# Relation-typed messages in a graph kernel: one-hots as the standing operand, weighted rows split in two fp32r parts, sums turned before they are added

## The reference, cut to what matters

```python
def _L1_gnn_ref(h, weight, norm, src, dst, rel_type):
    transformed = jnp.einsum('ni,rio->rno', h, weight)   # 16 relations
    msg = transformed[rel_type, src] * norm              # one row of 256 per edge
    return jax.ops.segment_sum(msg, dst, num_segments=h.shape[0])
```

## Time and profile before

| | us |
|---|---|
| median of 3 timed runs | 4358.07 (4357.03 to 4358.71) |
| span of the profiled execution | 4602.8 |
| of it from 2428 to 3597, the stage that is changed | 1169 |

### The profile page before, as it was taken

The page is one execution under the profiler, slowest core; times in us unless marked ns, Lnnn a source line. Parts: engine busy times, 40 slices in busy tenths (PEclk is TensorE's granted clock), DMA queues, the critical chain, the costliest instruction groups (busy, mean ns, idle before and its releaser), DMA issues. The chain is left out here.

```text
span 4602.8 us, 88005 instructions
## 1 busy us (share of the span) xinstructions
PE 3885.9 (84%) x23733; PEld 3489.0 (76%) x23733; DVE 2976.4 (65%) x7006; ACT 2107.0 (46%) x4811; POOL 2125.1 (46%) x2102
## 2 busy tenths in 40 slices
PE   7899999999999988989995666667666699999993
PEld 6798898989889877987885655556556578888883
DVE  7698898989889876554332222222321488989888
ACT  3565565656556536763221000000000288989882
POOL 0455555555555501000006666666666167667671
PEclk9899999999999987999995555665655599999996
DMA  4466666656556610004443333333333123323225
GB/s 138 135 176 171 171 175 171 177 170 175 169 170 177 169 31 23 24 26 161 151 150 103 89 87 89 92 87 91 87 89 90 52 55 75 63 67 70 60 48 120
DMA packets 226998, 509.09 MB, mean 111 GB/s; under 512 B 51805, under 2 KB 94299, under 8 KB 220426
## 3 DMA queue, kind: packets, MB, share of 16 engines
q0 software_dynamic: 116736, 313.66, 24.7%
q1 hardware_dynamic: 106389, 187.30, 14.6%
q10 hardware_dynamic: 3679, 5.79, 0.4%
HBM read 434.08 MB, written 72.49 MB: 110 GB/s over the span
## 5 line engine op out<-in xcount | busy, mean ns | idle before, releaser
L685 POOL DMA_INDIRECT big<-table,e_idx x784 | 751.2, 958 | 1049.6 <-DVE e_idx L721 649.0
L356 POOL DMA_INDIRECT big<-table,e_idx x784 | 767.0, 978 | 856.9 <-issue 304.1
L703 PE MATMUL psum<-e_near_hot,big 128*128 128x64 f32 x3136 | 621.9, 371 | 377.6 <-issue 361.9
L703 PEld LDWEIGHTS psum<-e_near_hot,big 128*128 128x128 f32 x3136 | 616.7, 292 | 391.7 <-issue 386.7
L2191 POOL DMA_INDIRECT g_S<-gsrc,g_idx x512 | 588.8, 1150 | 274.8 <-issue 157.8
L748 DVE TENSOR_TENSOR big<-big,psum 128x128 f32 x196 | 56.6, 289 | 801.9 <-remote 489.6
L435 ACT ACTIVATE e_hT_hi<-psum 128x256 fp32r<-128x256 f32 x784 | 300.2, 383 | 593.9 <-PE psum L375 513.1
L468 DVE TENSOR_TENSOR big<-psum,big 128x512 f32<-128x512 f32 x784 | 539.4, 688 | 45.5 <-issue 22.8
L386 PE MATMUL psum<-e_w_hi,e_hT_hi 128*128 128x256 f32 x1568 | 509.8, 325 | 0.3 <-issue 0.3
L386 PE MATMUL psum<-e_w_hi,e_hT_lo 128*128 128x256 f32 x1568 | 443.7, 283 | 0.0
L386 PE MATMUL psum<-e_w_lo,e_hT_hi 128*128 128x256 f32 x1568 | 440.7, 281 | 0.0
(11 more groups left out here) (397 smaller groups left out, 9090.5 us busy)
## 6 DMA issues: line engine op xcount, KB each, us to landing
big<-in_attr_t SPq DMA_DIRECT2D x392, 128.0 KB
g_rest<-gpart SPq DMA_DIRECT2D x128, 256.0 KB
big<-table,e_idx POOLq DMA_INDIRECT x1568
table<-C SPq DMA_DIRECT2D x26, 896.0 KB
table<-n_rows SPq DMA_DIRECT2D x24, 896.0 KB
experts<-g_region SPq DMA_DIRECT2D x15, 560.0 KB
g_S<-gsrc,g_idx POOLq DMA_INDIRECT x512
table<-big SPq DMA_DIRECT2D x25, 224.0 KB
```

Source lines behind the costliest of these rows:

```text
L356: pool.indirect_dma_start(G[:, j % 2, q, :], None, table, bass.IndirectOffsetOnAxis(idx[:, j, q:q + 1], 0)).then_inc(s[f"G_in{j % 2}{q}"], 16)
L685: pool.indirect_dma_start(G[:, j % n, q, :], None, c.table1, bass.IndirectOffsetOnAxis(idx[:, j, q:q + 1], 0)).then_inc(s[f"G_in{j % n}"], 16)
L703: last = pe.matmul(acc[:, b, :], G[:, j % n, q, b * 128:(b + 1) * 128], onehot[:, q, :], start=q == 0 and (b == 0 or s is sems[1]), stop=q ...
```

## The change

It changes only the first pass of `stage_relations` (the attention class gives up its own buffers for two weight matrices and takes them in `big`).

- The roles in the matmul are exchanged. The one-hot stands (128 edges x 64 nodes) and the gathered rows move (256 columns). Both are in fp32r, and as one fp32r value does not hold a weighted row exactly enough, the row is split in two: `hi` and `lo`. There are 8 matmuls a sup again (4 tiles x 2 parts).
- ScalarE makes `hi` = row x norm rounded to fp32r, 4 activations of 128x256 a sup. VectorE makes `lo` = row x norm - `hi`, 4 `scalar_tensor_tensor` of 128x256. Both have two buffers.
- The one-hot is no longer multiplied with `norm`; VectorE makes it two sups ahead, in 4 buffers.
- The sum now comes as nodes x features (64x256). ScalarE copies it out of PSUM (`rows`), TensorE turns it with two transposes, and VectorE adds the turned sum to `agg`.
- A slot of `G` is free again when `lo` has been made, not when the sup has been multiplied.
- `norm` is copied to a small tile (`scale`) with the indices.

The core of the diff:

```diff
-    NEAR_SLOTS, FAR_SLOTS, ACCS = 7, 2, 4
-    LEAD = 4
+    SLOTS, HOTS, FAR_SLOTS, FAR_BANKS = 7, 4, 2, 4
+    LEAD = 2
...
+        hi, lo = (sb(n, [128, 2, SUP, D], F32R) for n in ("hi", "lo"))
+        near_hot = sb("near_hot", [128, HOTS, SUP, WIN], F32R)
+        rows = c.C[0:WIN, 0:2, :]
...
+        def near_pool(pool):
...
+                    pool.wait_ge(s["low"], sup + 1)
...
+        def near_scalar(act):
+            def high(a):
+                k, j, sup = a
+                act.wait_ge(G_in[j % SLOTS], (k * (SUPS // SLOTS) + j // SLOTS + 1) * 16 * SUP)
+                act.wait_ge(s["sup_done"], sup + HOTS - 1)
...
+                for q in range(SUP):
+                    last = act.activation(hi[:, j % 2, q, :], G[:, j % SLOTS, q, :], ACT.Identity, scale=scale[:, j, q:q + 1])
+                last.then_inc(s["high"], 1)
+
+            def evict(a):
+                k, j, sup = a
+                act.wait_ge(s["sup_done"], sup + HOTS + 1)
+                act.wait_ge(s["turned"], sup + 1)
+                act.activation(rows[:, j % 2, :], acc(j), ACT.Copy).then_inc(s["rows"], 1)
             def step(k, v, beside=None):
+                if at(k, v - 2):
+                    evict(at(k, v - 2))
+                if at(k, v):
+                    high(at(k, v))
...
+        def near_tensor(pe):
+            def products(a, beside):
+                k, j, sup = a
+                pe.wait_ge(s["hot_ready"], sup + 1)
+                pe.wait_ge(s["low"], sup + SLOTS + 1)
+                pe.wait_ge(s["rows"], sup + 1)
+                for q in range(SUP):
+                    for n, part in enumerate((hi, lo)):
+                        last = pe.matmul(acc(j), near_hot[:, j % HOTS, q, :], part[:, j % 2, q, :],
+                                         start=q == 0 and n == 0, stop=q == SUP - 1 and n == 1)
...
+            def turn(a):
+                k, j, sup = a
+                pe.wait_ge(s["rows"], sup + 3)
+                pe.wait_ge(s["added"], sup + 1)
...
+                for b in range(KB):
+                    last = pe.transpose(turned(j)[:, b, :], rows[:, j % 2, b * 128:(b + 1) * 128], c.ident[0:WIN, 0:WIN])
+                last.then_inc(s["turned"], 1)
+            def step(k, v, beside=None):
+                if at(k, v):
+                    products(at(k, v), beside)
+                if at(k, v - 1):
+                    turn(at(k, v - 1))
...
+        def near_vector(dve):
...
+            def low(a):
+                k, j, sup = a
+                dve.wait_ge(s["high"], sup + 1)
+                for q in range(SUP):
+                    last = dve.scalar_tensor_tensor(out=lo[:, j % 2, q, :], in0=G[:, j % SLOTS, q, :], scalar=scale[:, j, q:q + 1],
+                                                    in1=hi[:, j % 2, q, :].bitcast(F32), op0=ALU.mult, op1=ALU.subtract)
+                last.then_inc(s["low"], 1)
+            def add_window(a):
+                k, j, sup = a
+                dve.wait_ge(s["turned"], sup + 3)
+                dve.wait_ge(s["added"], sup + 2)
...
+                dve.tensor_tensor(cols, cols, turned(j), ALU.add).then_inc(s["added"], 1)
+            def step(k, v, beside=None):
+                if at(k, v - 2):
+                    add_window(at(k, v - 2))
+                if at(k, v + LEAD):
+                    hots(at(k, v + LEAD))
+                a = at(k, v)
+                if a:
+                    low(a)
```

More of the change, by code:

```diff
@@ L649, in at, with far_loop, near_loop, acc @@
             return k, v, k * SUPS + v
[L651 to L676, removed]
+        def far_loop(eng, step, first):
+            for v in range(first, SUPS):
+                step(0, v)
+            with eng.Fori(1, NB - 1) as k:
+                for v in range(SUPS):
+                    step(k, v)
+            for v in range(SUPS + 1):
+                step(NB - 1, v)
+        def near_loop(eng, step, first, after, aside):
+            for v in range(first, SUPS):
+                step(0, v)
+            with eng.Fori(0, NT // GROUP) as g:
+                for v in range(SUPS):
+                    step(g + 1, v, lambda: aside(v % TURN, g, v // TURN, (g + 1) * SUPS + v))
+            for v in range(SUPS + after):
+                step(NB - 1, v)
+        def acc(j):
+            return c.ps[4 + j % 2][0:WIN, 0:D]
+        def turned(j):
+            return c.ps[6 + j % 2][:, 0:KB * WIN].rearrange("p (b n) -> p b n", b=KB)
+        def near_pool(pool):
             with pool.Fori(0, NB) as k:
@@ new lines, in far_acc, with far_pool @@
+        def far_acc():
+            return c.psum[:, 6:6 + KB, 0:FAR_WIN]
+        def far_pool(pool, p):
+            with pool.Fori(0, NB) as k:
+                for j in range(SUPS):
+                    sup = k * SUPS + j
+                    if j % TURN == 0:
+                        pool.wait_ge(f["idx_ready"], p * (2 * NB) + k * 2 + j // TURN + 1)
+                    pool.wait_ge(f["sup_done"], p * NSUP + sup + 1)
+                    pool.sem_inc(begun_gathering, 1)
+                    for q in range(SUP):
+                        pool.indirect_dma_start(G[:, j % FAR_SLOTS, q, :], None, c.table1,
+                                                bass.IndirectOffsetOnAxis(idx[:, j, q:q + 1], 0)).then_inc(far_in[j % FAR_SLOTS], 16)
@@ L693, in step, with far_tensor @@
+        def far_tensor(pe, p):
+            def step(k, v):
                 a = at(k, v)
@@ L747, in add_window, with step @@
                 c.fence(dve)
-                dve.tensor_tensor(cols, cols, acc, ALU.add).then_inc(s["added"], 1)
-            def step(k, v, beside=None):
-                a = at(k, v + lead)
+                dve.tensor_tensor(cols, cols, far_acc(), ALU.add).then_inc(f["added"], 1)
+            def step(k, v):
+                a = at(k, v + 1)
                 if a:
@@ L762, in step, with far_passes @@
                     indices(a[0] + 1, 0)
[L763 to L764 removed]
             indices(0, 0)
             indices(0, 1)
[L768 to L782 removed]
+            far_loop(dve, step, -1)
+            dve.wait_ge(f["added"], (p + 1) * NSUP + FAR_BANKS)
+            dve.tensor_scalar(rel[:, :], rel[:, :], -float(FAR_WIN), None, ALU.add).then_inc(f["shifted"], 1)
+            dve.wait_ge(f["shifted"], p + 1)
+        def far_passes(eng, one):
             more = eng.value_load(far_i[0:1, 0:1], min_val=0, max_val=1)
```

202 lines of the change are left out of this document (112 added, 90 removed).

## The result

The changed kernel takes 4574.51 us (median of 4 runs, 4567.11 to 4579.17) against 4358.39 (4 runs beside it, 4357.03 to 4360.94): ratio 1.0497, 95% interval 1.0482 to 1.0511, so 216 us slower. The forecast was 4520 with a range to 4590. The direction and the mechanism held, and the forecast was 54 us too low.

What follows compares the result with a forecast made beforehand. Gathers were taken to bound the old stage at 988 us, a TensorE-VectorE ring the new: 291 outside turns + 850 in turns + 13 at the ends = 1154, 166 more, so 4358 to 4524, said as 4520; range 4340 to 4590.

Steps and rivals of the forecast that it cites:

- The bound before: Changed stage before the change: GpSimd's gathers set the pace, 1.25 us each, 5.0 us a sup, 988 us undisturbed.
- The patches: Slow starts 2.1 us apart on TensorE and VectorE in the old profile: a recording cost, 181 us of the stage.
- rival D: All 245 us of profile excess lie in this stage: loss 230, time 4588; upper part of the forecast's 0.63.
- The ring: TensorE and VectorE alternate in the changed stage, neither working beside the other between low parts: 5.2 us a round.
- The bound of 5.6: Upper limit given for one TensorE-VectorE round in the changed stage, beside a lower 4.9 and the chosen 5.2 us.
- turn of 14 sups: Changed stage with attention blocks: 14 x 5.2 + 12.6 + 1.0 - 1.5 = 85 us, 6.1 us a sup.
- ScalarE: In the changed stage: 4 activations of 0.38 us and one copy, 2.0 us, running beside VectorE and TensorE.
- The clock: TensorE's granted clock in the changed stage stays down, at the half clock, outside short spells after attention blocks.
- B: Changed stage: the ring is shorter than the gathers' 5.0 us a sup, time 4368; chance 0.12.
- C: Changed stage: low parts and gathers lock each other out, each gather 0.42 us later, time 4679; chance 0.05.
- The signs I named: Changed stage: TensorE, VectorE and GpSimd waits, 5.2 us between additions, over 9 with a block, rare patches, profiled stage barely changed.
- rival A: The patches are real and TensorE bound the old stage: time 4343, or 4308 with a shorter ring; chance 0.20.

Runs made afterwards that it cites:

- the second trace: The kernel before, unchanged, profiled again: 4355.52 us, profiled span 4353.6 us.
- the swapped order: The changed kernel with VectorE making the low parts of v before it adds v-2, nothing else different: 4386.43 us, ratio 1.0066.
- the kernel before with the four additional instructions: The kernel before plus four VectorE instructions a sup in the form of the low parts, on constants, nobody else waiting for them: 4379.56 us, ratio 1.0034.

## Why the prediction was right, and where its sum was short

**The bound before.** Right: gathers at 1.25 us and 5.0 a sup (spacing 5.01; a gather fewer takes 1.25 off it, half the matmuls are worth 5 us). The undisturbed stage was 994 us from the first gather to the last addition, where I had 988.

**The patches.** Right that the timed runs don't pay them. Wrong in calling them the cost of recording as such, since the second recorded execution had none. It was one disturbed execution; what disturbed it stays open. Of its 249 us over the second trace 42 lay ahead of the stage (2429 against 2387), 173 in it and 34 behind, so the 181 of 245 that I gave to the stage were near, and rival D, with all of it there, was wrong in its mechanism although its 4588 came nearer than my 4520.

**The ring.** The mechanism is shown from three sides: cut by an order alone it vanishes (-188 us), VectorE's part lengthened adds 0.26 to 0.28 us to every sup (+54), TensorE's part shortened pays (-130) where it was worth 5 us before. The size was short:

| term, us | predicted | measured |
|---|---|---|
| low parts' end to the turn's end | 2.3 to 2.4 | 2.44 (0.10 + 2.34) |
| turn's end to the addition | 0.89 | 0.89 |
| addition to one-hot, to the first low part | 0.20, 0.33 | 0.20, 0.34 |
| four low parts | 1.42 | 1.66 |
| round outside the turns | 5.2 | 5.53 to 5.59 |
| turn of 14 sups | 85 | 89.6 |
| first gather to last addition | 1154 | 1221 |

The term that was mis-sized is the low parts, above all their spacing: 0.24 of the 0.37 us, some 47 us over 196 sups. I took 0.33 us from two neighbours of another form; with two inputs in SBUF and a scalar for each partition they start 0.40 apart, the four take 1.66 us, and one takes 478 ns where the edge stage's, with one input in PSUM and a constant in place of the scalar, takes 416. TensorE's part was 0.04 to 0.14 us longer than I had it. The bound of 5.6 that I gave for the round held. Over the 196 sups the round's 0.37 us is 73 us, of which the turn gives some back: in the turns a plain step is longer still (5.71), but the three blocks add 2.6, 2.7 and 4.0 us in the turn that I added up, and not 4.2 each, as part of the sup's own matmuls runs at the higher clock behind it, and it shortens the next step by up to 1 us. A turn of 14 x 5.72 + 9.3 - 1.7 = 87.7 us is what the first turn's steps add up to; the nine others, counted alike, take 88.7 to 90.9 (there two blocks in place of one can add 3.7 to 4.0 us, and in every second turn a step without a block takes 6.8). Stage: 56 x 5.57 (the mean of 5.59 and 5.56) = 312, 10 x 89.6 = 896, 13 at the ends, 1221. Against 994 that is +227 in the traces and +216 in the timed runs.

**ScalarE.** I had 0.38 us for an activation and it took 495 ns, with its input from SBUF and its scale from a tile. It cost nothing: ScalarE is a sup ahead, beside the ring.

**The clock.** It stayed down as forecast: 0.50 from 2428 to 2530, ahead of the turns, and 0.55 over the stage.

**The other rivals.** B (the ring shorter than the gathers' pace): no, but it describes the swapped order, which came out at 4386 for its 4368. C (low parts lock the gathers out): not in full, since no gather of the swapped order takes over 1.23 us; in a mild form it is real, 28 ns a gather on the mean, not 420. In the changed kernel the ring hides it.

**The signs I named.** The turn's wait, the matmul's wait, GpSimd's wait and the rare patches (none) came as said. A step with a block takes 8.3 to 9.8 us, where I had over 9. That the profiled stage would barely change did not: it grew by 52 us (1221 against 1169) where the sum had it shrink by 15, and these 67 us are the error of the sum.

**Slips in the working.** Seven starts at 0.22 us are 1.54 and not 1.65; the 2.3 to 2.4 for TensorE's part fits the 1.54. VectorE's own 3.2 us a sup comes out only with the 0.89 us ahead of the addition counted in; the rows alone give 2.1 to 2.4. In rival A 196 x 0.2 us is 39, so 4304 and not 4308. Rival A also has every stop of GpSimd put down to TensorE, but the earlier trace rows put down 41.1 us to TensorE and 137.5 to "remote". None of these moves the forecast.

## What to carry to other kernels

Before a change of an engine's instructions, ask which wait ends last in that stage: here GpSimd issued 784 gathers back to back, and half of TensorE's matmuls were worth 5 us. When two engines hand work to each other within one step, write down one round from wait to wait. Here VectorE's program put the use of an old result (the addition) ahead of the making of the next one (the low parts), and TensorE's put the turn that the addition needs behind the products that need the low parts. So all of it lay in one ring, though each of the two engines was idle for half of the time; the low parts moved ahead of the addition took back 188 of 216 us. And profile a kernel twice when its profiled span is well off its timed median.

## What the runs showed of the hardware

- An indirect gather costs GpSimd nearly a fixed time, on the mean 0.95 us with 128 rows of 1 KB, 0.96 with rows of 512 B and 0.91 with 64 rows, and 0.30 us between two.
- The gathers that had no VectorE instruction beside them took 945 to 948 ns in the three traces looked at (the kernel before again, the swapped order, the kernel before with the four additional instructions), also beside ScalarE's activations. Four VectorE instructions with two SBUF inputs a sup make the mean 28 ns longer (952 to 980). One more with a single SBUF input, beside the swapped order, raised it from 989 to 1005 ns.
- VectorE's `scalar_tensor_tensor` over 128x256 takes 478 ns with both inputs in SBUF and a scalar for each partition, and 416 with one input in PSUM and a constant (L481). Which of the two makes the difference was not tried; a `tensor_tensor` of this size takes 425 ns with both inputs in SBUF (L734 of the kernel before) and 422 with one in PSUM (L506), so the place of the input alone does little there.
- A ScalarE activation over 128x256 takes 495 ns from SBUF with a scale from a tile (L694), 406 from SBUF without one (a sigmoid, L442) and 384 from PSUM (a ReLU, L435).
- A burst of attention matmuls brought TensorE from a spacing of 0.21 us to 0.12 for the rest of the sup and for the next one, with a granted clock of 0.98 in place of 0.50. With half its matmuls left out in the kernel before, the stage had a granted clock of 0.56 against 0.59, and the time was within 5 us of the same.
